# First attention: products of split fp32r parts in pairs of tiles, softmax sums from a column of ones in V, more steps of overlap

## The reference

```python
mod = silu(c) @ ada_w.T + ada_b                 # six vectors of 256 for each sequence
h = layernorm(x) * (1 + scale_msa) + shift_msa
q, k, v = split(h @ qkv_w.T + qkv_b)            # 16 heads of 16 features
attn = einsum('bhnd,bhmd->bhnm', q, k) * 0.25
attn = softmax(where(mask, attn, -1e9))         # over the 64 keys of the sequence
out = einsum('bhnm,bhmd->bhnd', attn, v)
x = x + gate_msa * (out @ proj_w.T + proj_b)
```

## Time and profile before

| what | value |
|---|---|
| median of three runs | 2635.44 us (2632.98 to 2637.98) |
| the profiled execution's own time | 2634.42 us |
| its span, first to last instruction | 2631.4 us |
| busy: PE, DVE, ACT, POOL (whole span) | 92%, 74%, 59%, 39% |
| mean granted clock of PE | 0.965 of full speed |
| DMA queues, share of 16 engines | 8.8% and 4.0% |

### The profile page before, as it was taken

The page is one execution under the profiler, slowest core; times in us unless marked ns, Lnnn a source line. Parts: engine busy times, 40 slices in busy tenths (PEclk is TensorE's granted clock), DMA queues, the critical chain, the costliest instruction groups (busy, mean ns, idle before and its releaser), DMA issues. The chain is left out here.

```text
span 2631.4 us, 68381 instructions
## 1 busy us (share of the span) xinstructions
PE 2421.3 (92%) x25680; PEld 2099.8 (80%) x25680; DVE 1956.3 (74%) x3768; ACT 1546.6 (59%) x2913; POOL 1035.1 (39%) x872
## 2 busy tenths in 40 slices
PE   5999999969999989999999999999999923999997
PEld 4777777749999977888888888888888823899996
DVE  4888888856666657888888888888888857666663
ACT  3777777746666645555565555556555543555653
POOL 2667767730000013443344344334433402355544
PEclk9999999979999999999999999999999966999998
DMA  4111111000100110000000000000000021243332
GB/s 122 30 34 34 32 32 35 28 25 23 31 28 22 30 51 14 13 16 16 16 12 16 16 12 16 16 16 12 16 16 12 17 61 42 81 93 91 83 65 32
DMA packets 86352, 89.22 MB, mean 34 GB/s; under 512 B 26752, under 2 KB 80640, under 8 KB 83584
## 3 DMA queue, kind: packets, MB, share of 16 engines
q1 hardware_dynamic: 73984, 71.10, 8.8%
q0 software_dynamic: 12288, 17.05, 4.0%
HBM read 62.42 MB, written 25.69 MB: 33 GB/s over the span
## 5 line engine op out<-in xcount | busy, mean ns | idle before, releaser
L975 POOL TENSOR_TENSOR a_rq<-a_vq,minus_half 128x8 f32<-128x8 f32 x256 | 417.4, 1640 | 104.0 <-DVE a_vq L1000 104.0
L928 ACT ACTIVATE a_sq<-a_bqk 128x512 f32<-128x512 f32 x256 | 152.2, 595 | 345.8 <-PE a_bqk L126 345.8
L970 POOL TENSOR_TENSOR a_rstd<-a_veps,minus_half 128x1 f32<-128x1 f32 x64 | 35.3, 552 | 632.9 <-DVE a_veps L1044 632.9
L124 PE MATMUL a_bqk<-wqk_hi,a_h_lo 128*128 128x512 f32 x512 | 206.7, 404 | 5.1 <-DVE a_h_lo L1016 5.1
L125 PE MATMUL a_bqk<-wqk_lo,a_h_hi 128*128 128x512 f32 x512 | 201.4, 393 | 0.0
L126 PE MATMUL a_bqk<-wqk_hi,a_h_hi 128*128 128x512 f32 x512 | 201.3, 393 | 0.0
L992 DVE TENSOR_TENSOR a_qk<-a_bqk,a_rq 128x512 f32<-128x512 f32 x256 | 176.0, 688 | 29.7 <-POOL a_rq L975 29.5
L1725 DVE TENSOR_TENSOR e_u_lo<-e_u,e_u_hi 128x512 fp32r<-128x512 f32 x128 | 89.0, 696 | 126.7 <-ACT e_u_hi L1588 119.8
L124 PE MATMUL a_bb<-w_parts,a_o_lo 128*128 128x256 f32 x512 | 155.9, 305 | 27.2 <-DVE a_o_lo L1085 27.2
L920 ACT COPY a_vs<-a_ba 64x512 f32<-64x512 f32 x256 | 149.1, 582 | 53.5 <-PE a_ba L126 48.8
L1583 ACT ACTIVATE e_u<-e_bu,e_b 128x512 f32<-128x512 f32 x128 | 88.3, 690 | 156.7 <-PE e_bu L126 144.2
(11 more groups left out here) (259 smaller groups left out, 7825.6 us busy)
## 6 DMA issues: line engine op xcount, KB each, us to landing
X<-in_x SPq DMA_DIRECT2D x64, 128.0 KB
a_gate<-gates_of_rows SPq DMA_DIRECT2D x128, 64.0 KB, 2.5
m_gate<-gates_of_rows SPq DMA_DIRECT2D x32, 256.0 KB, 4.1
tokens<-a_xs SPq DMA_DIRECT2D x64, 128.0 KB, 1.7
out<-a_xs SPq DMA_DIRECT2D x64, 128.0 KB, 1.7
e_w<-in_fc1s SPq DMA_DIRECT2D x8, 1024.0 KB, 4.8
e_w<-in_fc2s SPq DMA_DIRECT2D x8, 1024.0 KB, 4.8
a_w<-in_fc_w SPq DMA_DIRECT2D x2, 1024.0 KB, 6.2
```

The source lines that it names most:

```text
L124: tensor.matmul(to, w_lo, x_hi, start=start, stop=False)
L928: nc.scalar.activation(sq[:, n * BK:(n + 1) * BK], b_qk[:, n * BK:(n + 1) * BK], ACT.Square).then_inc(s["sq"], 1)
L975: nc.gpsimd.tensor_tensor(rq[:, 8 * n:8 * n + 8], vq[:, 8 * n:8 * n + 8], g.mhalf[:, 0:8], ALU.pow).then_inc(s["rq"], 1)
```

## The change

1. **Split parts.** The weights of q, k, v and of the projection are split into two fp32r parts at the start of the stage (casts on ACT, subtractions on POOL). DVE splits hT into h_hi and h_lo, and o into o_hi (ACT) and o_lo (DVE). Each product becomes three of 256 columns.
2. **Pairs.** q and k are computed for two tiles at once, in even steps, into a bank each, and evicted for both tiles. DVE splits h in odd steps. v is computed with tokens on the partitions of its output, and evicted by four copies instead of two.
3. **Sums.** V gets a column of ones for each head (17 columns instead of 16), so P times V also yields the sums. The reduction over the keys goes; the reciprocal reads PSUM and stands right ahead of the division.
4. **Order.** DVE's step now begins with xhat of tile i+3 and the statistics of tile i+4, then o_lo (i-6), the split of h, masking, maximum and subtraction (i-1), and last reciprocal and division (i-5). PE's order is: q and k (even steps), a_o transposes (i-6), four transposes of P (i-3), xhat (i+2), scores (i-1), the other four transposes of P, P times V (i-4), v (i), projection (i-6). The transposes of P have one bank for both groups. The probabilities have four buffers. Steps run from -4 to 71 instead of -3 to 69.
5. **Loads.** SP loads X 14 tiles ahead. fc2's weights share the place of the stage's own weights, so their load waits until these are split.

The core of the diff (DVE and PE):

```diff
             @block.vector
             def _(dve):
                 def step(i, has, turn):
-                    if has(-4):
-                        dve.wait_ge(s["o"], i - 3)
...
-                        nc.vector.reduce_sum(sm[:, :], pb, AX).then_inc(s["summed"], 1)
-                        dve.wait_ge(s["summed"], i - 1)
...
+                    if has(3):
+                        dve.wait_ge(s["rstd"], i + 4)
...
+                        nc.vector.tensor_scalar(xhat[q][:, :], g.X[:, i + 3, :], mv[q][:, 0:1], rstd[q][:, 0:1],
                                                 ALU.subtract, ALU.mult).then_inc(s["xhat"], 1)
+                    if has(4):
...
+                    if has(-6):
+                        dve.wait_ge(s["o_hi"], i - 5)
+                        nc.vector.tensor_tensor(o_lo[:, :, :], b_pj[:, D:2 * D].rearrange("p (c q) -> p c q", c=DC),
+                                                o_hi[:, :, :].bitcast(F32), ALU.subtract).then_inc(s["o_lo"], 1)
+                    if has(2) and turn % 2 == 1:
+                        dve.wait_ge(s["hT"], i + 3)
+                        if later(i + 1) and has(-2):
+                            dve.wait_ge(s["v"], i - 1)
+                        nc.vector.tensor_copy(h_hi[:, pair, :, :], hT[:, :, :]).then_inc(s["h_hi"], 2)
+                        dve.wait_ge(s["h_hi"], i + 3)
+                        nc.vector.tensor_tensor(h_lo[:, pair, :, :], hT[:, :, :], h_hi[:, pair, :, :].bitcast(F32),
+                                                ALU.subtract).then_inc(s["h_lo"], 2)
                     if has(-1):
                         dve.wait_ge(s["s"], i)
...
+                    if has(-5):
+                        dve.wait_ge(s["o"], i - 4)
+                        heads = b_o[:, 0:H * HV].rearrange("p (h d) -> p h d", d=HV)
+                        nc.vector.reciprocal(rs[:, :], heads[:, :, HD0]).then_inc(s["recip"], 1)
+                        dve.wait_ge(s["recip"], i - 4)
...
+                        nc.vector.tensor_tensor(o_sb[:, :].rearrange("p (h d) -> p h d", h=H), heads[:, :, 0:HD0],
+                                                rs[:, :].unsqueeze(2).to_broadcast([P, H, HD0]), ALU.mult)\
+                            .then_inc(s["normed"], 1)
             @block.tensor
             def _(pe):
+                    if has(0) and turn % 2 == 0:
+                        pe.wait_ge(s["h_lo"], i + 2)
                         if later(i):
                             pe.wait_ge(s["q_out"], i)
+                        for to, off, done in ((b_k, DC, "k"), (b_q, 0, "q")):
+                            for n in range(DC):
+                                cols = slice((off + n) * P, (off + n + 1) * P)
+                                for kc in range(DC):
+                                    last = split_sum(nc.tensor, to[:, n * T2:(n + 1) * T2], wqkv_hi[:, kc, cols],
+                                                     wqkv_lo[:, kc, cols], h_hi[:, pair, kc, :], h_lo[:, pair, kc, :],
+                                                     n == 0 and kc == 0, kc == DC - 1)
+                            last.then_inc(s[done], 2)
+                    if has(-6):
+                        pe.wait_ge(s["normed"], i - 5)
...
+                    if has(-3):
+                        pe.wait_ge(s["exped"], i - 2)
+                        if later(i - 3):
+                            pe.wait_ge(s["pT_out"], 2 * (i - 3))
+                        turn_probs(0)
+                    if has(2):
+                        pe.wait_ge(s["xhat"], i + 3)
...
                     if has(-1):
                         pe.wait_ge(s["kbd"], i)
                         pe.wait_ge(s["q_out"], i)
...
                     if has(-3):
+                        pe.wait_ge(s["pT_out"], 2 * (i - 3) + 1)
+                        turn_probs(1)
+                    if has(-4):
...
+                    if has(0):
+                        if has(2):
+                            pe.wait_ge(s["hT"], i + 3)
...
+                            last = split_product(nc.tensor, b_vx[:, 0:D], h_hi[:, pair, kc, toks], h_lo[:, pair, kc, toks],
+                                                 wqkv_hi[:, kc, 2 * D:3 * D], wqkv_lo[:, kc, 2 * D:3 * D],
+                                                 kc == 0, kc == DC - 1)
+                        last.then_inc(s["v"], 1)
+                    if has(-6):
...
+                        pe.wait_ge(s["o_lo"], i - 5)
+                        for kc in range(DC):
+                            last = split_product(nc.tensor, b_pj[:, 0:D], o_hi[:, kc, :], o_lo[:, kc, :],
+                                                 wp_hi[:, kc, :], wp_lo[:, kc, :], kc == 0, kc == DC - 1)
                         last.then_inc(s["proj"], 1)
```

More of the change, by code:

```diff
@@ L307, in attention0_phase @@
         pbB = m.sb("a0_pbB", [P, D])
-        b_qk, b_vt = m.ps("a0_bqk", 4 * P), m.ps("a0_bvt", 4 * P)
-        VB = 4
+        b_q, b_k, b_vx = (m.ps("a0_b" + n, 4 * P) for n in ("q", "k", "vx"))
         b_s = m.ps("a0_bs", H * S)
[L311 to L315, removed]
+        b_pt = m.ps("a0_bpt", 4 * P)
+        b_o, b_pj = m.ps("a0_bo", 4 * P), m.ps("a0_bpj", 2 * D)
+        names = ("x_in stats aggr eps rstd xhat xT hT h_hi h_lo q k v q_out k_out kbd vm s scored maxed "
+                 "shifted exped recip pT pT_out o normed oT o_hi o_lo proj proj_out p1 p2 res gate pe_held dve_held "
+                 "w_in w_hi w_lo own_hi own_lo vb vb_mm pb").split()
         s = {n: m.sem("a0_" + n) for n in names}
         ident = g.cst[:, C_ID:C_ID + P]
+        wqkv_hi, wqkv_lo = g.own_hi, g.own_lo
         with nc.Block() as block:
@@ L363, in step @@
                         for c in range(DC):
[L364 to L368, removed]
+                            last = nc.scalar.activation(kT[:, c, :], b_k[:, c * T2:(c + 1) * T2], ACT.Identity,
+                                                        bias=g.qkb0[:, DC + c:DC + c + 1])
@@ L369, in step @@
+                        last.then_inc(s["k_out"], 2)
+                        act.wait_ge(s["q"], i + 2)
+                        if later(i) and later(i - 2):
+                            act.wait_ge(s["s"], i - 2)
                         for c in range(DC):
-                            last = nc.scalar.activation(qT[:, turn % 2, c, :], b_qk[:, c * P:(c + 1) * P], ACT.Identity,
+                            last = nc.scalar.activation(qT[:, pair, c, :], b_q[:, c * T2:(c + 1) * T2], ACT.Identity,
@@ L389, in step @@
[L389 to L396, removed]
@@ L397, in step @@
-                    if has(1):
-                        act.wait_ge(s["xT"], i + 2)
+                        last.then_inc(s["q_out"], 2)
+                    if has(-6):
+                        act.wait_ge(s["oT"], i - 5)
+                        nc.scalar.copy(o_hi[:, :, :], b_pj[:, D:2 * D].rearrange("p (c q) -> p c q", c=DC))\
+                            .then_inc(s["o_hi"], 1)
+                    if has(-3):
+                        turned_out(0)
+                    if has(2):
+                        act.wait_ge(s["xT"], i + 3)
+                        if first and later(i + 2):
+                            act.wait_ge(s["h_lo"], i + 2)
@@ L458, in step @@
[L458 to L469 removed]
+                    pa = pr[:, (turn - 1) % VB, :, :]
@@ L599, in _ @@
                 last.then_inc(s["vb_mm"], 1)
[L600 removed]
+                pe.wait_ge(s["own_lo"], 1)
+                pipeline_by(VB, pe, step, NT, 2, 8)
         m.clear()
```

279 lines of the change are left out of this document (141 added, 138 removed).

## The result

The changed kernel takes 3052.94 us (median of four runs, 3051.28 to 3054.82) against 2636.71 us for the kernel before in the same comparison: a ratio of 1.158, 95% interval 1.156 to 1.159. It is 416 us slower. The forecast was 2648, the range 2622 to 2680: slower was right, but the size was some thirty times too small (+13 forecast). The profiled execution's span is 3050.9 us (2631.4 before).

What follows compares the result with a forecast made beforehand. It took a DVE-to-PE round trip in the first attention as the bound: 15.60 + 0.69 + 0.06 = 16.35 us a pair, 8.175 a tile, 0.27 more; 59 tiles give +16, less 2, so 2648 us, range 2622 to 2680.

Steps and rivals of the forecast that it cites:

- The new round trip: First attention, DVE to PE and back: 7.02 us in even and 8.58 in odd steps, 15.60 a pair before collisions.
- The signs: First attention: DVE waiting for scores, PE idle before a_o transposes, PE 82% busy, steps near 9.3 and 7.1 us, stretched splits.
- circle open: First attention: round trip not closed, DVE's own 6.6 or PE's 6.7 us a tile bounds; 2562 us, chance 0.03.
- The clock: PE in first attention: were 1.2 GHz granted, 2.2 us would double, some +130, 2765 us; chance 0.03.
- The cast is excluded: Odd steps: DVE's cast of h waits for POOL's multiplication, the subtraction for its addition to X; 0.69 us lost.
- the first rival: No collision: DVE's cast isn't excluded or POOL's step lies elsewhere; 15.60 us a pair, 2626 us, chance 0.27.
- PE's own work: First attention after the change: 6.7 us a tile on PE, against 7.7 to 7.8 before.
- Start and end: Edges of the first attention: later first scores +3.5, short steps -7.5, last step -2, drain +4; sum -2 us.
- The short first steps: First four steps have no a_o transposes in the circle, each shorter by 1.9 us: -7.5.
- The gates' loads: SP loads the gates behind fc2, which waits for the weights' split; wanted 40 us later, so nothing.

Runs made afterwards that it cites:

- Experiment 2: The changed kernel with two banks for the output of P times V, q and k sharing one, division left last: 2678.0 us, ratio 1.016.
- experiment 1: The changed kernel with reciprocal and division moved from the end of DVE's step to its front: 2652.63 us, ratio 1.006.
- number 7: experiment 1 plus POOL building a_kbd before its operations on X and PE's order k, four P transposes, a_o transposes, q: 2588.7 us, ratio 0.982.
- experiment 3: The changed kernel with P times V moved to the end of PE's step, behind v and the projection: 2913.52 us in one run.

## Why the prediction was wrong

- **The step that failed** is the end of "The new round trip": "After the odd oT PE needs 0.36 + 0.51 + 0.37 + 1.03 + 0.51 + 1.05 + 0.69 + 0.69 + 2.76 = 7.97, less than 8.58". It lets P times V, v and the projection run beside DVE's masking and maximum. They can't in after: P times V waits for the division at the end of the same DVE step. I had followed the division's result forward, to the transposes of a_o, and not its other side, the release of b_o. The measured chain agrees with mine up to the division (masking to division 3.99 us, mine 4.00). From the division to oT I had 0.48; it is 5.73 in the even step (307.13 to 312.86). Behind the odd step's division (322.64) the 24 products of q and k stand in it too, and it is 8.17 (to 330.81). Experiment 2 takes this one wait away (a step then takes 8.51 us, forecast 8.175), and 375 of the 416 us go with it. So slower was right for a cause that makes a tenth of the loss at most.
- **The signs** that I had named for a right forecast mostly failed: PE was busy 60% of the time (82 forecast), odd and even steps were alike (14.87 and 14.72 us; 9.3 and 7.1 forecast), and PE's long wait stood before P times V. Only h_hi and h_lo were stretched as told.
- **The rival "circle open"** named the moment at which the division is waited for as the point that decides, and 2562 us as its price. In experiment 1 the division's place opens the circle; the time was 2653, because a_kbd and the transposes of a_o were late next. With these moved too it was 2589. So that rival's working lacked what waits next, as the forecast did.
- **The clock** had 0.03, for gaps of up to 1.8 us. The gaps were 4.2 and 6.75 us, and 108 us went that way. I had said 130, for 2.2 us of PE doubled in a circle of 8 us; here it is 1.72 us of a circle of 14 us, so that the two are near is luck. The chance hung on gaps that I had wrong. The Trainium skill (TensorE: Matmul & The Clock Gate, section "HAM oscillation — how this bites in real kernels") tells of a kernel whose PE falls back to the slow clock in each of its regular waits for a transfer; the trace agrees for a wait for DVE (0.74 with these gaps, 1.00 when they are filled).
- **The cast is excluded**, as the forecast assumed against the first rival: h_hi takes 1.00 us beside a_kbd (316.29) and 0.43 where POOL is idle (41.00), h_lo 1.34 against 0.69. It met a_kbd and not the multiplication, since everything had moved.
- **PE's own work** was sized rightly: 6.7 us a tile forecast; the best version has a period of 6.92 with PE 96% busy, 6.6 us.
- **Start and end.** The sum of -2 us was made of terms that must be compared one by one. The first scores were to come 3.5 us later; they came 6.2 later in after and 5.3 in number 7. The drain was to grow by 4; it grew by 15.7 and 9.4. The short first steps (-7.5) are real, but lie within the mean period: 28.9 us for four, where four later ones take 59. The gates' loads I had put at nothing. In number 7's drain (488 to 523 us) POOL waits for them six times, 11.9 us in all, before the multiplication; they have one buffer. What part of the 9.4 us this makes, no run separates.

## What to carry to other kernels

When an instruction is moved within its engine's step, follow both of its edges: who reads its result, and who waits to overwrite what it reads. A single PSUM bank between two engines can close a circle of its own. Here it helped to put the consumer that frees it at the front of its step, and nearly as much to take a second bank (the Trainium skill's Perfetto Trace Analysis, section "Matmuls", advises to rotate banks; experiment 2 agrees, with 8.31 us a tile against 14.18). When no engine is near full (61% at most here), look for two engines that each wait while the other works, before any duration is tuned.

## What the runs showed of the hardware

- Work that nobody uses can pay: the same 32 products of P times V took 1.93 us behind a gap and 1.13 behind unused products, and the stage became 1.72 us a tile faster by them (12.46 against 14.18).
- Which of DVE and POOL issued first decides who pays. In experiment 3 the subtraction was first and kept its 0.69, and a_kbd took 2.57 us; in number 7 a_kbd was first and the subtraction took 1.41:

```profile
305.32 0.69 DVE L507 TENSOR_TENSOR a_h_lo<-a_hT,a_h_hi 128x512 fp32r<-128x512 f32 x1
305.35 2.57 POOL L462 TENSOR_TENSOR a_kbd<-a_kT,consts_sb 128x512 f32<-128x512 f32 x2 [1.33 <-PE a_bs L609]
```

- An exclusion that stretched DVE's large subtraction by 0.2 us a tile (1435 against 1225 ns), at 95% busy, cost 0.04 us or less of the period, with PE at 96%; POOL's shorter operations gained some 8 us where the pipeline drained.
